# Second attention of a two-layer cross-attention kernel: score pieces, the maximum's transposition, the turned output and the projection placed elsewhere, and low parts of the probabilities moved from VectorE to GpSimd

## The chip, the core and the metric

The kernel runs on one core of one Trainium2 chip. The metric is the device time of one execution in microseconds. The engines are named as in the profile: PE (TensorE), DVE (VectorE), ACT (ScalarE), POOL (GpSimd), SP (the queue that issues the transfers). Each engine works through its own instructions in order; between engines only semaphores (`wait_ge`, `then_inc`) hold anything back.

## The reference, cut to what matters

Two layers are computed. The first has self-attention, cross-attention with 16 heads of 8, and a feed-forward part; nothing of it is changed. The second is one more cross-attention, over the same context, and it is the part that the change touches:

```
h = layernorm(x)                          # x: 16 batches x 56 queries x 128
Q = (h @ Wq).reshape(B, NQ, 16, 64)
K = (context @ Wk).reshape(B, NC, 16, 64) # context: 16 batches x 1500 keys x 96
V = (context @ Wv).reshape(B, NC, 16, 64)
attn = softmax(einsum('bihd,bjhd->bhij', Q, K)) * 64 ** -0.5
vals = einsum('bhij,bjhd->bihd', attn, V).reshape(B, NQ, 1024)
out = x + vals @ Wo + bo
```

## The kernel before

The second attention runs batch by batch, 16 batches. The 16 heads' queries (56 each) make 896 columns, 7 tiles of 128; the keys are 12 chunks of 125, two chunks to a group `g`, six groups and a seventh round for what is left. Wq and Wk are folded together beforehand, and Wv and Wo too, so that the context's 96 columns stand for keys and values both. `over_pairs` runs the batches in pairs, `par` 0 and 1 (a loop on the chip from the third batch to the fourteenth, the rest written out).

For batch `b`, PE does these things in a group `g`:

- **Scores** of two chunks, `score(i, par, u)`, four of them (L1319, L1320, 448 columns each), into four banks of PSUM, and then `score_rests` (L1328), which adds the last rows and subtracts the maximum. `score` u waits until ACT has read what lay in its bank (`n_exp`), four scores earlier.
- ACT takes the exponential from PSUM (L1423) into `P1`, four chunks deep.
- The **low part** of a chunk's probabilities, `Pl`, is `P1` minus its upper 16 bits. Before, POOL makes it (L1300) for all chunks but 3, 7 and 11, which are DVE's (L1521). Either reads two tensors that lie in SBUF.
- **Values** of the two chunks of the group before, `values` (L1346 to L1348, 21 products per chunk), which wait for the low part (`n_low_p`, `n_low_d`).
- Beside it, **pieces** for the next batch: its scores are computed once roughly (L1033, 21 pieces of 128 x 500), only for their maxima, which DVE reduces (L1042). Two PSUM banks alternate, so a piece waits until the piece two before it is reduced (`n_red`). Row `g` of the table `PLACES` says where pieces stand in group `g`: after the first, second and third score, after the rests, and after each chunk's values.

At a batch's end (g = 6) DVE makes the next batch's maximum (`negate_maximum`, L1487 to L1495: a reduction and four tiny instructions on 128 x 7, all in SBUF, one after the other), PE transposes it (`turn_maximum`, L1373), then does the values of chunks 10 and 11; DVE lays the maximum into the next batch's queries (L1501), which that batch's fourth score waits for.

The finished batch's output is divided by its sums by DVE (`finish_batch`, L1453 and L1457, at the start of the next batch), turned by PE (`turn_output`, L1357, two parts), kept by ACT (L1440) and DVE (L1466), and, once for two batches (`par` 0), projected by PE (`project`, L1365, 48 products) and finished by DVE (`finish_tile`, L1471 and L1475). POOL also makes the low part of the next batch's context once per batch (`cNl`, L1304), after chunk 3's place.

Of the kernel before, what the change touches and what calls it, by code (L numbers as in the profile page):

```python
# [37 lines left out]
SK, DC = 1500, 96  # L38
# [74 lines left out]
def program(nc, table, x, ctx_768, w_qkv, b_qkv, w_so, b_so, w_q, b_q, w_k, b_k, w_v, b_v, w_co, b_co,  # L113
            w1, b1, w2, b2, w3, b3, ln_g, ln_b, Wq, Wk, Wv, Wo, bo, gamma, beta, out):
    with ExitStack() as ctx:
# [1119 lines left out]
        mn1 = sb_in(late, "mn1", [128, MR])  # L1235
# [6 lines left out]
        PLACES = [(0, 0, 0, 0, 0, 0), (0, 0, 0, 0, 0, 1), (1, 1, 1, 1, 1, 1), (1, 0, 1, 1, 1, 1), (1, 0, 1, 1, 1, 1), (1, 1, 1, 1, 0, 0), (0,) * 6]  # L1242
# [3 lines left out]
        n_mready, n_mturned, n_mlaid = (sem(n) for n in ("n_mready", "n_mturned", "n_mlaid"))  # L1246
# [4 lines left out]
        low_on_dve = [c % 4 == 3 for c in range(NC)]  # L1251
# [13 lines left out]
        with nc.Block() as block:  # L1265
# [42 lines left out]
            def _(pe):  # L1308
# [23 lines left out]
                def values(i, par, c, tiles):  # L1332
                    n = i * 2 + par
                    if tiles[0] == 0:
                        if low_on_dve[c]:
                            pe.wait_ge(n_low_d, n * DV + sum(low_on_dve[:c + 1]))
                        else:
                            pe.wait_ge(n_low_p, n * (NC - DV) + c + 1 - sum(low_on_dve[:c + 1]))
                        if c == 0:
                            pe.wait_ge(n_cnl, n + 1)  # L1340
                            wait_for(pe, n_on, n)
# [10 lines left out]
                def turn_output(n, k):  # L1352


                    pe.wait_ge(n_on, n + 1)
                    for t in range(4 * k, min(4 * k + 4, QT)):
                        mm = pe.transpose(PS[0:DC, W1[k], (t % 4) * 128:(t % 4 + 1) * 128], On[:, t, :], ident)  # L1357
                    mm.then_inc(n_oturned, 1)
# [10 lines left out]
                def turn_maximum(i, par):  # L1369
                    n = i * 2 + par + 1  # L1370
                    pe.wait_ge(n_mready, n + 1)
                    for first in (32, 96):
                        mm = pe.matmul(PS[first:first + MR, W1[0], 0:128], mn1[:], ident, start=True, stop=True)  # L1373
                    mm.then_inc(n_mturned, 1)

                def body(i, par):
# [10 lines left out]
                    for g in range(NG + 1):  # L1387
                        if has_1 and g == NG:
                            turn_maximum(i, par)
                        if has_b and g < NG:  # L1390
                            for j in range(2 * GC):
                                score(i, par, 2 * GC * g + j)
                                if has_old and g == 1 and j < 2:
                                    turn_output(b - 1, j)
                                if j < 3:
                                    pieces(g, j)
                            score_rests(par, g)
                        pieces(g, 3)
                        for j in range(GC):
                            if has_b and g > 0:  # L1400
                                values(i, par, GC * (g - 1) + j, tuple(range(QT)))
                            pieces(g, 4 + j)
                        if has_b and has_old and par == 0 and g == 1:
                            project(i - 1)
# [42 lines left out]
            def _(dve):  # L1447
                def finish_batch(n):
# [5 lines left out]
                    dve.wait_ge(n_r, n * 2 + 2)  # L1454
                    wait_for(dve, n_oturned, n * 2)
                    for k in range(2):
                        m = nc.vector.scalar_tensor_tensor(out=On[:, 4 * k:4 * k + 4 - k, :], in0=o[k][:, :, 0:DC], scalar=SCALE1,  # L1457
                                                           in1=spread(r7[:, 4 * k:4 * k + 4 - k], 2, DC), op0=ALU.mult, op1=ALU.mult)
                    m.then_inc(n_on, 1)
# [17 lines left out]
                def body(i, par):  # L1477
# [6 lines left out]
                    def negate_maximum():  # L1484
# [9 lines left out]
                        nc.vector.tensor_scalar(mn1[:, 0:QT], mh1[:], -1.0, None, ALU.mult)  # L1494
                        nc.vector.tensor_tensor(mn1[:, QT:], mh1[:], mt1[:], ALU.subtract).then_inc(n_mready, 1)  # L1495
# [10 lines left out]
                    for g in range(NG + 1):  # L1506
# [4 lines left out]
                        if has_b and has_old and par == 0 and g == 2:  # L1511
                            finish_tile(i - 1)
# [4 lines left out]
                        if has_b and g >= 2 and g % 2 == 0:  # L1517
# [38 lines left out]
```

## Time and profile before

| | us |
|---|---|
| median of 3 runs | 1120.08 (1120.08 to 1121.38) |
| the profiled execution | 1121.01, of it the span of the profile 1119.1 |
| feed-forward part and preparation | 480 to 583 |
| second attention, batches | 583 to 1107 |
| its last output and projection | 1107 to 1119 |
| mean granted clock of PE over the span | 0.969 of full speed |

Every start time is counted in microseconds from the start of the span. A matmul's duration in the trace is that of one passing through the array, and successive ones overlap: for a stream of them the distance of two starts is what one costs. Idle time that the trace gives before a matmul is counted from the end of the one before, so start-to-start it is some 0.2 us more. A row with "x4" merges four instructions in a row on that engine.

### The profile page before, as it was taken

To read this page: it belongs to the slowest core of one execution; us is meant where nothing else is said; L and a number is where in the kernel's file an instruction comes from. 1 tells how busy PE (TensorE), PEld (TensorE's weight loads), DVE (VectorE), ACT (ScalarE), POOL (GpSimd) and SP (SyncE) were. 2 spreads that over 40 slices of the span, in tenths; PEclk is the share of its full clock that TensorE was granted. 3 is DMA by queue.
4 is the path that set the end of the run, shared out by engine and by line. 5 is a ranking of instruction groups with operands and counts; after the bars stand their busy time and mean duration, and the time that the engine had idled before them with its cause. 6 is when DMAs were issued, how large, how long until landed. Compare 5 with 4: busy or idle time off the path is not lost. (4 is left out here: it accounts for less than half of the span.)

```text
span 1119.1 us, 31806 instructions
## 1 busy us (share of the span) xinstructions
PE 1016.2 (91%) x12092; PEld 704.7 (63%) x12092; DVE 752.5 (67%) x1409; ACT 543.3 (49%) x1139; POOL 402.6 (36%) x290
## 2 busy tenths in 40 slices
PE   5977899999999999889678999999999999999997
PEld 2652577777677776646326676766766666676666
DVE  4646778887888788221786667677676767766662
ACT  2533577677776776631443434333443442444442
POOL 4821121112111123020115545445555544655543
PEclk9988899999999999989799999999999999999998
DMA  3501444444344533020023122222022222112200
GB/s 111 136 1 63 141 140 132 130 150 138 123 130 146 145 107 90 19 80 1 0 76 93 45 77 75 54 75 71 27 72 74 59 68 75 48 48 73 57 2 4
DMA packets 54605, 88.31 MB, mean 79 GB/s; under 512 B 10850, under 2 KB 39348, under 8 KB 54548
## 3 DMA queue, kind: packets, MB, share of 16 engines
q1 hardware_dynamic: 54548, 87.52, 26.6%
q8 instruction: 40, 0.66, 0.3%
q14 instruction: 17, 0.14, 0.0%
HBM read 57.27 MB, written 21.96 MB: 71 GB/s over the span
## 5 line engine op out<-in xcount | busy, mean ns | idle before, releaser
L1423 ACT ACTIVATE P<-PS 125x448 f32<-125x448 f32 x384 | 177.8, 550 | 309.2 <-PE PS L1328 309.2
L1300 POOL TENSOR_TENSOR Pl<-P 125x896 f16<-125x896 f32 x144 | 240.7, 1686 | 239.9 <-ACT P L1423 239.5
L1042 DVE TENSOR_REDUCE m<-PS 128x1 f32<-128x500 f32 x336 | 216.1, 675 | 92.7 <-PE PS L1033 91.0
L922 DVE TENSOR_REDUCE m_part<-PS 128x1 f32<-128x500 f32 x336 | 210.5, 672 | 55.2 <-PE PS L824 53.7
L900 ACT ACTIVATE Pb<-PS 125x448 f32<-125x448 f32 x384 | 186.1, 549 | 19.8 <-PE PS L799 18.8
L1346 PE MATMUL PS<-cNh,P 125*128 125x97 f16 x1344 | 186.3, 208 | 1.1 <-POOL Pl L1300 1.1
L1348 PE MATMUL PS<-cNh,Pl 125*128 125x97 f16 x1344 | 185.7, 207 | 0.0
L1347 PE MATMUL PS<-cNl,P 125*128 125x96 f16 x1344 | 185.5, 206 | 0.0
L1319 PE MATMUL PS<-qA,kA 128*125 128x448 f16 x384 | 136.7, 356 | 8.5 <-ACT P L1423 8.2
L1347 PEld LDWEIGHTS PS<-cNl,P 125*128 125x128 bf16 x1344 | 132.0, 98 | 11.5
L1346 PEld LDWEIGHTS PS<-cNh,P 125*128 125x128 bf16 x1344 | 131.5, 98 | 11.3 <-issue 9.5
L775 POOL TENSOR_TENSOR Qst<-Qspace,tab 96x224 f16<-96x224 f32 (+1 forms) x64 | 33.7, 556 | 290.7 <-DVE Qst L962 281.6
L824 PE MATMUL PS<-KH,Qmx 128*128 128x500 f16 x336 | 129.8, 388 | 8.7 <-DVE m_part L922 4.2
L1033 PE MATMUL PS<-kA,qA 96*128 96x500 f16 x336 | 126.9, 378 | 9.3 <-DVE m L1042 7.8
L1320 PE MATMUL PS<-qB,kB 128*125 128x448 f16 x384 | 134.9, 351 | 0.0
L1348 PEld LDWEIGHTS PS<-cNh,Pl 125*128 125x128 f16 x1344 | 131.4, 98 | 0.0
L799 PE MATMUL PS<-Qst,Kst 110*125 110x224 f16 x768 | 110.9, 263 | 4.9 <-DMA Kst<-k_halves 2.1
L799 PEld LDWEIGHTS PS<-Qst,Kst 110*125 110x125 f16 x768 | 87.8, 137 | 30.4 <-ACT Pb L900 7.7
L810 PE MATMUL PS<-Pb,Vst 125*32 125x112 f32 x3072 | 93.3, 262 | 0.0
L810 PEld LDWEIGHTS PS<-Pb,Vst 125*32 125x32 f32 x3072 | 70.4, 109 | 19.6 <-issue 15.4
L1319 PEld LDWEIGHTS PS<-qA,kA 128*125 128x125 f16 x384 | 52.2, 136 | 30.1 <-ACT P L1423 15.4
L1521 DVE TENSOR_TENSOR Pl<-P 125x896 f16<-125x896 f32 x48 | 61.2, 1276 | 14.0 <-ACT P L1423 14.0
(170 smaller groups left out, 1522.7 us busy)
## 6 DMA issues: line engine op xcount, KB each, us to landing
Kst<-k_halves SPq DMA_DIRECT2D x144, 125.0 KB, 2.8
k_halves<-KH SPq DMA_DIRECT2D x16, 750.0 KB, 3.3
cx<-in_ctx SPq DMA_DIRECT2D x16, 562.5 KB
d_cx<-in_ctx SPq DMA_DIRECT2D x16, 562.5 KB
kB<-c_halves SPq DMA_DIRECT2D x32, 187.5 KB, 3.3
c_halves<-cHi SPq DMA_DIRECT2D x16, 281.2 KB, 2.7
c_halves<-cLo SPq DMA_DIRECT2D x16, 281.2 KB, 3.0
kA<-c_halves SPq DMA_DIRECT2D x16, 281.2 KB, 3.2
```

Source lines behind the costliest of these rows:

```text
L799: mm = pe.matmul(PS[0:KC, u % 3, (g % 2) * 224:(g % 2 + 1) * 224], Kst[:, par, g, c * KC:(c + 1) * KC], Qst[:, par, g, :], start=True, sto ...
L810: mm = pe.matmul(PS[32 * (p % 4):32 * (p % 4) + 32, OB, (p // 4) * TP:(p // 4 + 1) * TP], Vst[:, par, c, p, :], Pb[:, c % NPB, p * TP:(p + ...
L900: nc.scalar.activation(Pb[:, c % NPB, half * HALF:(half + 1) * HALF], PS[0:KC, u % 3, 0:HALF], ACT.Exp, scale=SCALE0).then_inc(exp_done, 1)
L922: nc.vector.tensor_reduce(m_part[:, t, part:part + 1], PS[:, 6 + k % 2, 0:SP], AX.X, ALU.max).then_inc(s_reduced, 1)
L1042: nc.vector.tensor_reduce(m21[:, t, part:part + 1], PS[:, banks[k % 2], 0:SP], AX.X, ALU.max).then_inc(n_red, 1)
L1300: nc.gpsimd.tensor_tensor(Pl[:, c % NP], P1[:, c % NP], high, ALU.subtract).then_inc(n_low_p, 1)
L1319: pe.matmul(o, kA[:, par, at], qA[:, par, cols], start=True, stop=False)
L1320: pe.matmul(o, kB[:, par, at], qB[:, par, cols], start=False, stop=True)
L1346: pe.matmul(o, high, cNh[:, par, c, :], start=(c == 0 and t % 4 == 0), stop=False, skip_group_check=True)
L1347: pe.matmul(o[:, 0:DC], high, cNl[:, par, c, :], start=False, stop=False, skip_group_check=True)
L1348: mm = pe.matmul(o, Pl[:, c % NP, cols], cNh[:, par, c, :], start=False, stop=(c == NC - 1), skip_group_check=True)
L1423: nc.scalar.activation(P1[:, c % NP, half * HALF:(half + 1) * HALF], PS[0:KC, u % 4, 0:HALF], ACT.Exp).then_inc(n_exp, 1)
```

## The change

Seven things are changed, all in the second attention:

1. DVE keeps only chunk 3's low part; those of chunks 7 and 11 are POOL's.
2. `PLACES` for groups 2 and 3 are exchanged: group 2 has five pieces and group 3 six.
3. `turn_maximum` is one product with 128 rows of output in place of two with 14 each; `mn1` is therefore 128 x 2 x 64, cleared once, and the last two tiny instructions of `negate_maximum` write 128 x 2 x 7.
4. `turn_output` stands between group 0's rests and group 1's first score, both parts together, in place of within group 1's scores.
5. `finish_batch` signals each half of the output for itself, and `turn_output` waits for its own half.
6. `project` stands after the values of chunk 0, in place of after chunk 1's and the first piece.
7. `finish_tile` stands in group 1 ahead of the first piece's reduction, in place of in group 2.

```diff
-        mn1 = sb_in(late, "mn1", [128, MR])
+        mn1 = sb_in(late, "mn1", [128, 2, 64])
-        PLACES = [(0, 0, 0, 0, 0, 0), (0, 0, 0, 0, 0, 1), (1, 1, 1, 1, 1, 1), (1, 0, 1, 1, 1, 1), (1, 0, 1, 1, 1, 1), (1, 1, 1, 1, 0, 0), (0,) * 6]
+        PLACES = [(0, 0, 0, 0, 0, 0), (0, 0, 0, 0, 0, 1), (1, 0, 1, 1, 1, 1), (1, 1, 1, 1, 1, 1), (1, 0, 1, 1, 1, 1), (1, 1, 1, 1, 0, 0), (0,) * 6]
-        low_on_dve = [c % 4 == 3 for c in range(NC)]
+        low_on_dve = [c == 3 for c in range(NC)]
...
                 def turn_output(n, k):
-                    pe.wait_ge(n_on, n + 1)
+                    pe.wait_ge(n_on, n * 2 + k + 1)
...
                     pe.wait_ge(n_mready, n + 1)
-                    for first in (32, 96):
-                        mm = pe.matmul(PS[first:first + MR, W1[0], 0:128], mn1[:], ident, start=True, stop=True)
-                    mm.then_inc(n_mturned, 1)
+                    pe.matmul(PS[:, W1[0], 0:128], mn1[:].rearrange("p a c -> p (a c)"), ident, start=True, stop=True).then_inc(n_mturned, 1)
...
                                 score(i, par, 2 * GC * g + j)
-                                if has_old and g == 1 and j < 2:
-                                    turn_output(b - 1, j)
                                 if j < 3:
                                     pieces(g, j)
                             score_rests(par, g)
+                        if has_b and has_old and g == 0:
+                            turn_output(b - 1, 0)
+                            turn_output(b - 1, 1)
                         pieces(g, 3)
                         for j in range(GC):
                             if has_b and g > 0:
                                 values(i, par, GC * (g - 1) + j, tuple(range(QT)))
+                            if has_b and has_old and par == 0 and g == 1 and j == 0:
+                                project(i - 1)
                             pieces(g, 4 + j)
-                        if has_b and has_old and par == 0 and g == 1:
-                            project(i - 1)
...
-                    dve.wait_ge(n_r, n * 2 + 2)
                     wait_for(dve, n_oturned, n * 2)
                     for k in range(2):
-                        m = nc.vector.scalar_tensor_tensor(...)
-                    m.then_inc(n_on, 1)
+                        dve.wait_ge(n_r, n * 2 + k + 1)
+                        nc.vector.scalar_tensor_tensor(...).then_inc(n_on, 1)
...
-                        nc.vector.tensor_scalar(mn1[:, 0:QT], mh1[:], -1.0, None, ALU.mult)
-                        nc.vector.tensor_tensor(mn1[:, QT:], mh1[:], mt1[:], ALU.subtract).then_inc(n_mready, 1)
+                        nc.vector.tensor_scalar(mn1[:, :, 32:32 + QT], spread(mh1[:], 1, 2), -1.0, None, ALU.mult)
+                        nc.vector.tensor_tensor(mn1[:, :, 32 + QT:32 + MR], spread(mh1[:], 1, 2), spread(mt1[:], 1, 2), ALU.subtract).then_inc(n_mready, 1)
...
-                        if has_b and has_old and par == 0 and g == 2:
+                        if has_b and has_old and par == 0 and g == 1:
                             finish_tile(i - 1)
...
-                        if has_b and g >= 2 and g % 2 == 0:
+                        if has_b and g == 2:
```

At a batch's end, inside the loop, DVE's instructions stood like this before (`m` are the piece maxima, `mt`, `mh`, `mn` the steps of the maximum, `Pl` the low part of chunk 11, `qC` the next batch's queries):

```order
L1042 TENSOR_REDUCE m<-PS 128x1
L1487 TENSOR_REDUCE mt<-m 128x7
L1489 TENSOR_SCALAR mt<-mt 128x7
L1491 CAST mh<-mt 128x7
L1494 TENSOR_SCALAR mn<-mh 128x7
L1495 TENSOR_TENSOR mn<-mh,mt 128x7
L1521 TENSOR_TENSOR Pl<-P 125x896
L1501 TENSOR_TENSOR qC<-PS,tab 14x512 x2
```

and now like this:

```order
L1042 TENSOR_REDUCE m<-PS 128x1
L1488 TENSOR_REDUCE mt<-m 128x7
L1490 TENSOR_SCALAR mt<-mt 128x7
L1492 CAST mh<-mt 128x7
L1495 TENSOR_SCALAR mn<-mh 128x2x7
L1496 TENSOR_TENSOR mn<-mh,mt 128x2x7
L1502 TENSOR_TENSOR qC<-PS,tab 14x512 x2
```

The low part of chunk 11 has left DVE, where it stood behind the maximum's four tiny instructions. On POOL the second attention's first two batches read so (`Pl` the low parts, `cNl` that of the context; the sign says which kernel):

```order
 L1300 TENSOR_TENSOR Pl<-P 125x896 x3
 L1304 TENSOR_TENSOR cNl<-d_cx,cNh 125x1152
-L1300 TENSOR_TENSOR Pl<-P 125x896 x9
+L1300 TENSOR_TENSOR Pl<-P 125x896 x11
 L1304 TENSOR_TENSOR cNl<-d_cx,cNh 125x1152
-L1300 TENSOR_TENSOR Pl<-P 125x896 x6
+L1300 TENSOR_TENSOR Pl<-P 125x896 x8
```

The run behind each `cNl` is longer by two, the low parts of chunks 7 and 11, and chunk 11's now stands directly behind chunk 10's. On PE the start of a batch in the loop, from group 0's rests on, stood so before (`On` is the divided output, turned):

```order
L1328 MATMUL PS<-qC,kC 125x448 x4
L84 REGISTER_ALU
L1319 MATMUL PS<-qA,kA 125x448
L1320 MATMUL PS<-qB,kB 125x448
L1357 MATMUL PS<-tab,On 96x128 x4
L84 REGISTER_ALU
L1319 MATMUL PS<-qA,kA 125x448
L1320 MATMUL PS<-qB,kB 125x448
L1357 MATMUL PS<-tab,On 96x128 x3
```

and now:

```order
L1328 MATMUL PS<-qC,kC 125x448 x4
L1355 ISA
L1357 MATMUL PS<-tab,On 96x128 x4
L1355 REGISTER_ALU
L1357 MATMUL PS<-tab,On 96x128 x3
L84 REGISTER_ALU
L1319 MATMUL PS<-qA,kA 125x448
L1320 MATMUL PS<-qB,kB 125x448
```

The seven transpositions now stand ahead of group 1's first score.

## Rows read from the trace of the kernel before

**Rows 1.** Windows: PE, PEld, DVE, ACT, POOL busy us (x instructions), PEclk, DMA share, GB/s.
```profile
583.00:1107.00 524.00, 492.17 (x6004) 351.39 (x6004) 350.51 (x605) 210.75 (x461) 277.47 (x160) 1.00 0.21 60
```

**Rows 2.** Waits of PE, all of the span: us in total, times, longest.
```profile
PE PS L1373 <- DVE mn L1495: 18.5, 16, 2.5
...
PE PS L1319 <- ACT P L1423: 8.2, 16, 0.5
PE PS L1033 <- DVE m L1042: 7.8, 21, 0.7
```

**Rows 3.** Timeline of DVE at one batch's end (start, us, engine, line, instruction).
```profile
744.95 1.42 DVE L1489 TENSOR_SCALAR mt<-mt 128x7 f32<-128x7 f32 x1
746.40 0.17 DVE L1491 CAST mh<-mt 128x7 f16<-128x7 f32 x1
...
746.69 0.16 DVE L1495 TENSOR_TENSOR mn<-mh,mt 128x7 f32<-128x7 f16 x1
```

**Rows 4.** Timeline of POOL, then of ACT, at that end and the next start.
```profile
744.66 1.68 POOL L1300 TENSOR_TENSOR Pl<-P 125x896 f16<-125x896 f32 x1 [1.93 <-ACT P L1423]
752.28 3.32 POOL L1300 TENSOR_TENSOR Pl<-P 125x896 f16<-125x896 f32 x2 [5.94 <-ACT P L1423]
...
743.61 1.85 ACT L1423 ACTIVATE P<-PS 125x448 f32<-125x448 f32 x4 [3.40 <-PE PS L1328]
```

**Rows 5.** Timeline of PE, same stretch.
```profile
746.90 0.40 PE L1373 MATMUL PS<-tab,mn 128*14 128x128 f32 x4 [1.09 <-DVE mn L1495]
747.24 0.22 PE L1346 MATMUL PS<-cNh,P 125*128 125x97 f16 x1
...
751.82 0.40 PE L1319 MATMUL PS<-qA,kA 128*125 128x448 f16 x1 [0.54 <-ACT P L1423]
...
752.25 0.60 PE L1357 MATMUL PS<-tab,On 128*96 128x128 f32 x4
...
755.68 0.21 PE L1346 MATMUL PS<-cNh,P 125*128 125x97 f16 x1
```

**Rows 6.** Lines L1489 and L1521: duration ns min/median/max, first and last start.
```profile
L1489 DVE TENSOR_SCALAR mt<-mt x16: 171/1415/1417, 582.4 to 1076.7; 128x7 f32<-128x7 f32 x16
L1521 DVE TENSOR_TENSOR Pl<-P x48: 1079/1082/2107, 595.2 to 1104.1; 125x896 f16<-125x896 f32 x48
```

**Rows 7.** Timeline of DVE, POOL and PE in that next batch, group 2.
```profile
758.87 2.10 DVE L1521 TENSOR_TENSOR Pl<-P 125x896 f16<-125x896 f32 x1
...
757.73 2.30 POOL L1304 TENSOR_TENSOR cNl<-d_cx,cNh 125x1152 f16<-125x1152 f32 x1 [0.23 <-ACT cNh L1427]
...
761.62 0.39 PE L1033 MATMUL PS<-kA,qA 96*128 96x500 f16 x1 [0.68 <-DVE m L1042]
```

**Rows 8.** Timeline of POOL and DVE at 18 us, and line L358.
```profile
18.30 3.57 POOL L358 TENSOR_TENSOR Kbd<-SKT,tab 128x896 f32<-128x896 f32 x2 [9.27 <-DVE SKT L430]
...
18.66 1.67 DVE L434 SCALAR_TENSOR_TENSOR wkv<-wkv 97x256 f16<-97x256 f32 x1
...
L358 POOL TENSOR_TENSOR Kbd<-SKT,tab x16: 1689/1692/1866, 18.3 to 58.1; 128x896 f32<-128x896 f32 x16
```

**Rows 9.** Timeline in a batch with a projection: PE, then DVE.
```profile
725.53 0.35 PE L1320 MATMUL PS<-qB,kB 128*125 128x448 f16 x1
725.88 0.39 PE L1033 MATMUL PS<-kA,qA 96*128 96x500 f16 x1
...
726.07 0.29 DVE L1475 TENSOR_TENSOR Z<-Y,X 112x128 f32<-112x128 f32 x1 [0.24 <-DVE Y L1471]
```

**Rows 10.** Timeline of DVE behind the last batch.
```profile
1107.36 0.92 DVE L1457 SCALAR_TENSOR_TENSOR On<-PS,r 128x384 f32<-128x384 f32 x2
```

**Rows 11.** Windows around long gaps of PE, columns as in rows 1.
```profile
560.00:583.00 23.00, 17.50 (x48) 5.23 (x46) 21.73 (x41) 8.24 (x15) 0.00 (x0) 1.00 0.18 49
...
95.00:112.00 17.00, 10.90 (x28) 2.71 (x27) 14.32 (x23) 4.05 (x5) 3.75 (x5) 0.77 0.30 106
...
1107.00:1119.00 12.00, 6.35 (x56) 5.89 (x55) 3.04 (x10) 1.08 (x4) 0.00 (x0) 0.67 0.03 7
```

More of the change, by code:

```diff
@@ L1245, in program @@
         n_cn, n_cnl = sem("n_cn"), sem("n_cnl")
-        n_mready, n_mturned, n_mlaid = (sem(n) for n in ("n_mready", "n_mturned", "n_mlaid"))
+        n_mzero, n_mready, n_mturned, n_mlaid = (sem(n) for n in ("n_mzero", "n_mready", "n_mturned", "n_mlaid"))
         n_exp, n_low_d, n_low_p, n_pv = (sem(n) for n in ("n_exp", "n_low_d", "n_low_p", "n_pv"))
@@ L1340, in values @@
                             pe.wait_ge(n_cnl, n + 1)
-                            wait_for(pe, n_on, n)
+                            wait_for(pe, n_on, n * 2)
                     for t in tiles:
@@ L1447, in _ @@
             def _(dve):
+                nc.vector.memset(mn1[:], 0.0).then_inc(n_mzero, 1)
+                dve.wait_ge(n_mzero, 1)
                 def finish_batch(n):
@@ L1453, in finish_batch @@
                         nc.vector.reciprocal(r7[:, 4 * k:4 * k + 4 - k].unsqueeze(2), o[k][:, :, DC:DC + 1]).then_inc(n_r, 1)
-                    dve.wait_ge(n_r, n * 2 + 2)
                     wait_for(dve, n_oturned, n * 2)
                     for k in range(2):
-                        m = nc.vector.scalar_tensor_tensor(out=On[:, 4 * k:4 * k + 4 - k, :], in0=o[k][:, :, 0:DC], scalar=SCALE1,
-                                                           in1=spread(r7[:, 4 * k:4 * k + 4 - k], 2, DC), op0=ALU.mult, op1=ALU.mult)
-                    m.then_inc(n_on, 1)
+                        dve.wait_ge(n_r, n * 2 + k + 1)
+                        nc.vector.scalar_tensor_tensor(out=On[:, 4 * k:4 * k + 4 - k, :], in0=o[k][:, :, 0:DC], scalar=SCALE1,
+                                                       in1=spread(r7[:, 4 * k:4 * k + 4 - k], 2, DC), op0=ALU.mult, op1=ALU.mult).then_inc(n_on, 1)
                 def split_old(i, par, k):
```

## The prediction

> **What bounds the kernel now.** I read the windows first, then PE's waits, then the timeline of one batch's end and the next one's start. Through the 524 us of the second attention PE is busy 492 us, at the full granted clock (1.00), while DVE has 351 and POOL 277 [rows 1]. So PE's stream bounds the stretch, and the time changes where PE stands still, or where its stream gets shorter. The list of its waits names three places that the change touches [rows 2]: the maximum's transposition (16 times, 18.5 us), the first score of group 1 behind ACT's exponential (16 times, 8.2 us), and a piece behind DVE's reduction (21 times, 7.8 us). Everything is at one of these.
>
> Why does the first one exist? At a batch's end DVE subtracts a constant from 128 x 7 numbers (L1489). That took 1.42 us, from 744.95 to 746.37 [rows 3], but 171 ns the first time, at 582.4, when POOL did nothing; the median of its 16 is 1415 ns [rows 6]. POOL's low part of chunk 10 ran from 744.66 to 746.34 [rows 4]: DVE's tiny instruction ended 0.03 us after POOL's. The 1.42 us are not work, they are a wait for POOL. The reader is to see the same at two other places. DVE's low part of chunk 3 takes 1082 ns as a rule and 2107 at most [rows 6]; the one at 758.87 took 2.10, and POOL's `cNl` beside it ran until 760.03 [rows 7]. And at 18.66 a DVE instruction with two inputs in SBUF took 1.67 us: it ended at 20.33, soon after the first of two POOL instructions in a row (18.30, 3.57 us both) must have ended, and before the second did [rows 8]. One of POOL's L358 took 1866 ns against a median of 1692 [rows 8]: DVE, having waited, was let in between, and POOL's second was held up a little.
>
> **The change part by part.** All against the profiled execution, 1121.01 us (span 1119.1), which is 0.93 over the median 1120.08.
>
> *Chunk 11's low part to POOL.* Its input is there early: ACT ends all four exponentials at 743.61 + 1.85 = 745.46 [rows 4]. So POOL starts it as soon as chunk 10's ends, 746.34, and two in a row take 3.32 us [rows 4]; this one ends at about 744.66 + 3.32 = 747.98, say 748.02 with L1489 let in between. Before, POOL was idle from 746.34 until 752.28 [rows 4], and in that idle time DVE did the cast and the two instructions that write `mn` (746.40 to 746.85), and PE its transposition at 746.90 [rows 3, 5]. Now these meet a busy POOL. L1489 gets in at 746.37 as before; the cast comes 0.03 us later [rows 3], POOL has started again, and the cast ends at 748.02 + 0.03 = 748.05. From its end to the end of L1495 is 746.85 - 746.57 = 0.28 us [rows 3], so `mn` is ready at 748.33 and PE starts at 748.38 instead of 746.90: **+1.48 us a batch**. Bounds: no row shows that cast beside POOL. If it and the scalar instruction slip through, the last one, L1496, still has two SBUF inputs as L1521 has, whose wait is shown [rows 6, 7]; it would end at about 748.05 in place of 746.85: +1.2. If L1489 is not let in between but has to wait for both, the chain starts at 748.02 and needs 746.85 - 746.37 = 0.48: +1.65. If nothing waits, 0 (a rival below). I take 1.48, because the cast is nearest to L1489: one input, both sides in SBUF, seven elements. PE has nothing ahead of this wait to do: chunk 10's and 11's values and the whole next batch stand behind it on PE, and ACT's exponentials behind those. DVE's laying of the maximum and its low part no longer stand between, but the fourth score that waits for them is more than 2 us behind, so their leaving DVE gives nothing. The same goes for chunk 7's low part: PE does not wait in groups 4 and 5, before or after.
>
> [...]
>
> *One transposition for two.* From the first product's start to chunk 10's first value is 747.24 - 746.90 = 0.34 us for four passes [rows 5]; with two passes some 0.11 less, and loading 128 columns instead of 14 takes back a little: **-0.10 us a batch** (0 to -0.12).
>
> So a batch's end costs +1.38, fifteen times (the transposition ahead of the first batch meets an idle POOL, 171 ns): **+20.7 us**, between 15 x 1.08 = 16.2 and 15 x 1.55 = 23.3. In the last batch there is no maximum, but chunk 11's low part, 1.66 us behind chunk 10's, is later than chunk 10's values (21 products, 0.91 us) need it: **+0.7**.
>
> *The turned output before group 1.* PE waited 0.54 us ahead of group 1's first score and then spent 7 x 0.11 = 0.77 us on transpositions between scores [rows 5]; with restart costs the gap was 0.65. Now the transpositions lie in it: chunk 11's values end at 747.24 + 1.82 = 749.06 [rows 5], DVE's divisions (0.92 us [rows 10], 0.5 behind that) are done by 750.5, and PE comes at 751.82 - 0.6 = 751.2. PE is 0.65 us early at the end of group 1's scores. What is late next is POOL: the low parts of chunks 0 and 1 ran 752.28 to 755.60 [rows 4] and start with ACT's exponential, which didn't move. In a batch without a projection chunk 1's values began at 755.68 [rows 5], 0.08 after that; they can begin at 755.65 now. So there the gain is **0.03**. In a batch with a projection its 2.7 us now stand between chunk 0's values and chunk 1's and cover that wait; the gain of 0.65 stays.
>
> *finish_tile in group 1.* After the projection a piece came 0.35 us after the score ahead of it in place of 0.19 [rows 9]: 0.17 us of waiting for Y. Now Y is made beside chunk 1's values. But Z reads two SBUF tensors [rows 9], and beside POOL's `cNl` it can wait a microsecond; the reductions behind it are late then, and piece 2 by some 0.1. Together a batch with a projection gains 0.65 + 0.17 - 0.1 = **0.7, seven times: -4.9 us** (bounds 0.4 and 0.82).
>
> *Five pieces in group 2.* In batches without a projection PE waited 0.84 us start to start (0.68 idle) at 761.62, since L1521 had stood waiting for `cNl` [rows 7], and 0.05 at an earlier piece. ACT's copy for `cNl` now starts 0.6 us earlier, and `cNl` goes behind three low parts in a row (755.60 + 1.68 = 757.28) until about 759.5; L1521 comes at 759.2, waits 0.3 and ends at 760.5, and chunk 3's values want it at 760.7. With five pieces instead of six the last one, at 761.6, needs a reduction that ends at 761.1. Group 3's sixth piece finds DVE caught up. So the wait goes: **-0.89, with the 0.03 -0.92, seven times (the last batch has no pieces): -6.4 us** (bounds 0.3 and 0.95).
>
> *The tail.* The first half of the last output is signalled 0.4 us earlier of its 0.92 [rows 10]: **-0.4**. The clearing of `mn1` is hidden: it is 128 elements during the first batch's preparations.
>
> Sum: 20.7 + 0.7 - 4.9 - 6.4 - 0.4 = **+9.7**. From 1121.01 that is 1130.7; against the median, **1129.8 us**.
>
> **The rivals.**
> - *The tiny instructions slip past POOL*, because DVE is served at each handover or these sizes don't contend. For it: L1489 did get in behind a POOL instruction. Against: it got in only where POOL ended, and L1521 with two inputs never ran beside POOL's work. Then the end of a batch gives -0.10 x 15 = -1.5, and the sum is -1.5 + 0.7 - 4.9 - 6.4 - 0.4 = -12.5: 1107.6. It decides from the point where the added wait is below 0.76 us a batch. Chance 0.10.
> - *The gains are eaten as well*: low parts come later still for group 2 (POOL has 11 of them and `cNl` now, three in a row at the start), so L1521 waits behind `cNl` as before and nothing is won in batches without a projection, half in the others: 20.7 + 0.7 - 2.5 - 0.4 = +18.5, 1138.6. Chance 0.07.
> - *The clock falls.* PE's idle time per batch's end grows from 1.09 [rows 5] to some 2.5 us. For it: in 95 to 112 us, with PE busy 10.90 of 17, the mean granted clock was 0.77, and behind the last batch 0.67 [rows 11]. Against: in 560 to 583, with PE busy 17.50 of 23, it was 1.00 [rows 11], and a batch here would be busy nine tenths. If it fell for some 3.4 us each time, half of that is lost: 15 x 1.7 = +25, 1155. Chance 0.03.
> - *It nets to nothing*: only L1496 waits, and the earlier parts give their upper bounds: 16.2 + 0.7 - 5.7 - 6.7 - 0.6 = +3.9, 1124. Chance 0.08, a third of it within no change.
>
> **How the numbers follow.** The forecast has 0.72. Its own range is 1125.5 to 1133; the tail's projection runs at a clock that is partly halved (0.67), which may shift by a microsecond or two either way. The range reaches down to the case of a part wait and up towards eaten gains: 1123 to 1138. A measurement of this kernel can tell 0.2% (2.2 us) from no change. Faster is 0.12, no change 0.04, slower 0.84.
>
> **What would show it.** Right: after, L1492 (the cast) or what is behind it takes 1.4 to 1.7 us and ends with POOL's second low part; PE's wait ahead of L1372 sums to about 18.5 + 15 x 1.48 = 40 us; the wait at group 1's first score is gone in all batches but the first; in batches without a projection a new wait of 0.6 us for POOL stands at chunk 1's values, and the piece at 761.62 no longer waits. Wrong: the cast and L1496 stay at 0.17 us beside a busy POOL (then 1107), or PEclk below 1.00 between 583 and 1107 (then over 1140), or L1522 in group 2 still at 2.1 us in batches without a projection.

## The result: slower by 2.5 %, and the profile after

| | before | after |
|---|---|---|
| median us | 1120.08 (1118.76 to 1121.38, 4 runs) | 1148.06 (1147.05 to 1149.92, 4 runs) |
| ratio | 1 | 1.0252 [1.0233, 1.027] |
| profiled execution, its span | 1121.01, 1119.1 | 1147.42, 1145.5 |
| mean granted clock of PE | 0.969 | 0.957 |

The forecast was 1129.8 with a range to 1138, so the sign is right and the size is not: +28.0 us in place of +9.7. The views of after, in the order in which I read them. First PE's waits, which answer to [rows 2]:

```profile
PE PS L1372 <- DVE mn L1496: 40.4, 16, 2.7
...
PE PS L1346 <- POOL Pl L1300: 4.7, 11, 0.7
...
PE PS L1033 <- DVE m L1042: 3.1, 14, 0.7
```

The wait ahead of the transposition has gone from 18.5 to 40.4 us, where 40 was forecast. At group 1's first score a single wait of 0.5 us for ACT is left (16 waits, 8.2 before), and the pieces wait less (3.1 against 7.8). The timelines of one batch's end, DVE, POOL and PE, answer to [rows 3 to 5]:

```profile
751.43 0.17 DVE L1488 TENSOR_REDUCE mt<-m 128x7 f32<-128x21 f32 x1
751.64 1.42 DVE L1490 TENSOR_SCALAR mt<-mt 128x7 f32<-128x7 f32 x1
753.09 1.60 DVE L1492 CAST mh<-mt 128x7 f16<-128x7 f32 x1
754.73 0.17 DVE L1495 TENSOR_SCALAR mn<-mh 128x14 f32<-128x14 f16 x1
754.81 0.17 DVE L1496 TENSOR_TENSOR mn<-mh,mt 128x14 f32<-128x14 f16 x1
```
```profile
751.35 3.32 POOL L1300 TENSOR_TENSOR Pl<-P 125x896 f16<-125x896 f32 x2 [1.93 <-ACT P L1422]
```
```profile
755.04 0.49 PE L1372 MATMUL PS<-tab,mn 128*128 128x128 f32 x2 [2.53 <-DVE mn L1496]
755.36 0.21 PE L1346 MATMUL PS<-cNh,P 125*128 125x97 f16 x1
```

POOL's two low parts run from 751.35 to 754.67. L1490 ends at 753.06, about where the first must have ended (751.35 + 1.68 = 753.03); the cast, which took 0.17 us before, takes 1.60 and ends at 754.69, 0.02 after POOL's second. PE stands idle for 2.53 us in place of 1.09. L1490 and the cast wait for semaphores of DVE's own steps alone, and for none of POOL's, so "only semaphores hold anything back" does not hold for these two engines here: L1490 took 1.42 us and the cast 1.60, where each took 0.17 with no POOL instruction beside it (L1490 in e6, the cast in before). So far this is the mechanism of the prediction. The windows show what it left out; they answer to [rows 1]:

```profile
583.00:1133.00 550.00, 506.46 (x5943) 367.30 (x5943) 337.95 (x571) 207.89 (x459) 325.60 (x192) 0.96 0.20 57
719.50:722.90 3.40, 3.40 (x35) 3.00 (x33) 1.80 (x6) 0.00 (x0) 0.00 (x0) 0.50 0.43 120
722.90:753.00 30.10, 29.61 (x356) 21.13 (x354) 18.86 (x31) 13.11 (x29) 18.81 (x12) 1.00 0.11 34
```

The mean granted clock of the second attention is 0.96, not 1.00. The second row is 3.4 us right behind a batch's end: PE busy throughout, granted clock 0.50; the third, the rest of that batch, is at 1.00. Such a stretch of 3.4 us goes with 12 of the 15 transpositions at a batch's end in the profiled execution: it begins between the transposition's start and 1.2 us behind it. (One more begins behind the last batch, where before had one too.) By estimate, with half of each 3.4 us lost at 0.50, that is 12 x 1.7 = 20.4 us. At three ends with the same standstill, at 755.04, 894.99 and 1034.92, the clock did not fall; they lie four batches apart.

### The profile page after: what moved, and what is told of

It reads as the page before. It is cut to its first block and busy times, and to the rows that moved or that the text cites. A ratio compares the mean times of both kernels' runs of the same rounds, so it can differ in the third digit from the quotient of the medians.

```text
span 1145.5 us, 31762 instructions
## 1 busy us (share of the span) xinstructions
PE 1029.2 (90%) x12060; PEld 719.2 (63%) x12060; DVE 741.2 (65%) x1378; ACT 542.0 (47%) x1139; POOL 452.8 (40%) x322
## 5 line engine op out<-in xcount | busy, mean ns | idle before, releaser
L1300 POOL TENSOR_TENSOR Pl<-P 125x896 f16<-125x896 f32 x176 | 291.6, 1679 | 224.1 <-ACT P L1422 224.1
L1346 PE MATMUL PS<-cNh,P 125*128 125x97 f16 x1344 | 200.5, 215 | 4.7 <-POOL Pl L1300 4.7
L1348 PE MATMUL PS<-cNh,Pl 125*128 125x97 f16 x1344 | 200.1, 214 | 0.0
L1347 PE MATMUL PS<-cNl,P 125*128 125x96 f16 x1344 | 199.7, 213 | 0.0
L900 ACT ACTIVATE Pb<-PS 125x448 f32<-125x448 f32 x384 | 185.9, 547 | 19.5 <-PE PS L799 18.5
L1347 PEld LDWEIGHTS PS<-cNl,P 125*128 125x128 bf16 x1344 | 137.6, 102 | 12.3
L1346 PEld LDWEIGHTS PS<-cNh,P 125*128 125x128 bf16 x1344 | 136.9, 102 | 13.0 <-POOL Pl L1300 11.7
L1319 PE MATMUL PS<-qA,kA 128*125 128x448 f16 x384 | 139.3, 363 | 0.8 <-ACT P L1422 0.5
L1320 PE MATMUL PS<-qB,kB 128*125 128x448 f16 x384 | 137.2, 357 | 0.0
L1348 PEld LDWEIGHTS PS<-cNh,Pl 125*128 125x128 f16 x1344 | 136.8, 102 | 0.0
L1320 PEld LDWEIGHTS PS<-qB,kB 128*125 128x125 f16 x384 | 53.8, 140 | 20.3
```

The source lines that it names most:

```text
L900: nc.scalar.activation(Pb[:, c % NPB, half * HALF:(half + 1) * HALF], PS[0:KC, u % 3, 0:HALF], ACT.Exp, scale=SCALE0).then_inc(exp_done, 1)
L1300: nc.gpsimd.tensor_tensor(Pl[:, c % NP], P1[:, c % NP], high, ALU.subtract).then_inc(n_low_p, 1)
L1319: pe.matmul(o, kA[:, par, at], qA[:, par, cols], start=True, stop=False)
L1320: pe.matmul(o, kB[:, par, at], qB[:, par, cols], start=False, stop=True)
L1346: pe.matmul(o, high, cNh[:, par, c, :], start=(c == 0 and t % 4 == 0), stop=False, skip_group_check=True)
L1347: pe.matmul(o[:, 0:DC], high, cNl[:, par, c, :], start=False, stop=False, skip_group_check=True)
```

## The experiments

The distance from one maximum's transposition to the next gives the length of a batch, in us, for batches with a projection (`par` 0) and without. It is the finest measure here, since the runs of one kernel differ by up to 8 us (e1: 1103.42 to 1111.71) while these lengths repeat within 0.03 us in the loop as long as the clock doesn't fall:

| kernel | with | without | median us | ratio to before |
|---|---|---|---|---|
| before | 34.16 | 32.21 | 1120.08 | 1 |
| after | 36.45 | 34.33 (32.71 without a fall) | 1148.06 | 1.0252 |
| e1 chunk 11 back to DVE | 33.43 | 31.28 | 1108.65 | 0.9908 [0.9891, 0.9925] |
| e2 before, chunk 11 to POOL | 35.6 to 37.1 | 35.25 | 1161.88 | 1.0372 [1.0355, 1.0389] |
| e4 transposition later | 33.96 | 31.81 | 1116.84 | 0.9971 [0.9961, 0.9982] |
| e10 one product in the gap | 34.86 | 32.71 | 1128.69 | 1.0074 [1.0051, 1.0097] |
| e7 e1, output's places of before | 34.16 | 31.62 | 1115.59 | 0.9959 [0.9947, 0.9972] |
| e8 e1, pieces' places of before | 33.81 | 31.67 | 1114.00 | 0.9949 [0.9936, 0.9962] |
| e6 e1, chunk 10 on DVE too | 32.97 | 30.82 | 1100.52 | 0.9814 [0.9797, 0.9831] |
| e11 e6, some of chunk 1 too | 32.97 | 30.59 | 1098.07 | 0.9806 [0.9786, 0.9827] |

The theory: chunk 11's low part on POOL makes DVE's cast wait (+1.48 a batch), and PE's longer standstill makes the clock fall. The rivals: the fall has another source, or the gains of the other edits are missing.

**e1 and e2, the one move undone, and the one move alone.** Of after, then of before:

```diff
-        low_on_dve = [c == 3 for c in range(NC)]
+        low_on_dve = [c in (3, 11) for c in range(NC)]
...
-                        if has_b and g == 2:
+                        if has_b and g in (2, 6):
```


> The changed kernel with chunk 11's low part given back to DVE, behind the maximum's tiny instructions; all other edits stay. Theory A (GpSimd's low part of chunk 11, right behind chunk 10's, holds up the maximum's cast by 1.43 us, and the longer standstill of TensorE lets the granted clock fall): the cast is back at 0.17 us, TensorE's wait ahead of the maximum's transposition is back from 40.4 to 18.5 us in total, the granted clock is 1.00 from 583 us on, and the time is about 1109 us (1120 less the 11 us that the other edits were worked out to give). Theory B (the clock falls because of another of the edits, such as the 128-row transposition or the pieces' places): the wait is back, but the clock stays at 0.96 there and the time is about 1131 us. Theory C (GpSimd is overloaded with eleven low parts): chunk 7's alone keeps half of the loss, about 1130 us.


```diff
-        low_on_dve = [c % 4 == 3 for c in range(NC)]
+        low_on_dve = [c in (3, 7) for c in range(NC)]
...
-                        if has_b and g >= 2 and g % 2 == 0:
+                        if has_b and g in (2, 4):
```


> The kernel before with one thing changed: chunk 11's low part goes to GpSimd, chunks 3 and 7 stay on VectorE. Theory A: the cast takes 1.6 us in 15 batches, TensorE's wait ahead of the transposition goes from 18.5 to about 40 us, which gives 1120 + 22 + 0.7 = 1143 us, and the clock falls at nearly every batch's end too, another 20 us or so: about 1163 us. Theory B: the wait grows but the clock stays at 1.00, because other edits let it fall: 1143 us. Theory C: nearly nothing, 1120 to 1125 us.

Measured 1108.65 and 1161.88. The cast's line, PE's waits and the windows of e1:

```profile
L1492 DVE CAST mh<-mt x16: 172/173/174, 580.0 to 1063.1; 128x7 f16<-128x7 f32 x16
...
PE PS L1372 <- DVE mn L1496: 18.9, 16, 2.7
...
583.00:1090.00 507.00, 485.74 (x5922) 349.32 (x5922) 332.08 (x586) 207.74 (x459) 299.19 (x175) 1.00 0.21 61
```

and of e2:

```profile
L1491 DVE CAST mh<-mt x16: 174/1606/1607, 584.0 to 1116.6; 128x7 f16<-128x7 f32 x16
...
PE PS L1373 <- DVE mn L1495: 40.0, 16, 2.5
...
583.00:1150.00 567.00, 511.01 (x6004) 368.00 (x6004) 356.93 (x597) 211.64 (x461) 303.82 (x176) 0.96 0.19 56
```

The move alone gives the before kernel the long cast, the 40 us of waiting and the clock of 0.96; without it none of the three is there, and the other six edits, with chunk 7's low part still on POOL, gain 0.9 %. The whole loss comes with chunk 11's move.

**e3, e5, e9: fill the gap, keep the cast late.** Products whose results nobody reads (e3's are added to 97 columns beside the accumulators, in their bank, which hold no result) stand ahead of the transposition's wait: 54 of 97 columns, 12 of 448 columns, or three float32 ones of 448 columns.

```diff
+                    if inside(i, par, 0):
+                        pe.wait_ge(n_exp, (i * 2 + par) * 2 * NC + 2 * NC - 3)
+                        for _ in range(3):
+                            pe.matmul(PS[0:KC, 0, 0:HALF], ident[0:KC, 0:KC], P1[:, 9 % NP, 0:HALF], start=True, stop=True)
                     pe.wait_ge(n_mready, n + 1)
```


> The changed kernel with 54 more products (128 x 97, into columns of a PSUM bank that nobody reads) on TensorE ahead of the wait for the maximum, 54 x 0.043 = 2.3 us a batch, so that TensorE works through most of the 2.7 us in which it stood still. Nothing else moves. Theory A: the added work costs nothing, the cast still takes 1.6 us, the granted clock is 1.00 from 583 us on, and the time is 1148 less 13 falls of 3.4 us at half speed (1.7 us each) = about 1126 us, within 1124 to 1130. Theory B (the clock falls for another reason): the clock stays at 0.96 and the time at 1148 us or above.

> The changed kernel with 12 long extra products (96 x 448, into a score bank that is free then, result unread) ahead of TensorE's wait for the maximum: 12 x 0.19 = 2.3 us a batch, in 12 instructions in place of the 54 of the run before. With 54, the falls of the clock at the batches' ends were gone, but TensorE stood still 3.3 to 3.6 us for nothing the profile names at the loop's first score, five times, and the clock fell there. Theory A (the standstill makes the clock fall; the new one came from the longer program in the loop): no such standstill with 12, the clock 1.00 from 583 us on, the wait for the maximum below 0.5 us each, and 1148 - 22 = about 1126 us (1124 to 1130). Theory B (the clock falls for another reason): 1148 us.

> The changed kernel with three extra float32 products (125 x 448, 0.76 us each by the float32 products of the feed-forward part, result unread) ahead of TensorE's wait for the maximum: 2.3 us a batch in three instructions. The loop's program on TensorE then has 883 instructions in place of 875; with 901 and 983 it was loaded anew in each pass and TensorE stood still for about 4 us. Theory A (the standstill lets the clock fall; the loop's size is what cost the other two runs their gain): no loading in the loop, the clock 1.00 from 583 us on, 1148 - 22 = about 1126 us. Rival (883 is already too long): loading and 5 standstills of 4 us again, about 1150 us. Theory B (the clock falls for another reason): 1148 us with the clock at 0.96.

Measured 1154.51, 1159.56 and 1159.48: all slower than after. The first two are a plain miss; e9 went the way of its rival (a loop that is too long, about 1150), and beyond it. The falls at the batches' ends were gone, but something new had come. PE's waits, a row of PE's timeline, and the page's instruction queue of e9:

```profile
PE PS L1319 <- issue: 20.6, 5, 4.5
...
792.83 0.63 PE L1319 MATMUL PS<-qA,kA 128*125 128x448 f16 x1 [4.43 <-issue]
...
q8 instruction: 85, 1.39, 0.6%
```

At the loop's first score PE stands still five times, named only "issue": 3.6 to 4.5 us in e9, up to 4.0 in e5 and up to 3.6 in e3. The clock falls at each: over the 12 us behind the standstill its mean is 0.75 to 0.88. The queue that carries instructions has 85 packets (87 in e3) where before and after have 40. The times of these three therefore say nothing of the gap. The lengths of their other batches do: 34.86 and 32.71, with PE idle for at most 0.26 us ahead of the transposition and no fall (clock 1.00). Why the five standstills are there became a question of its own (below).

**e10, the gap filled with one instruction.** As e9, with one product (0.76 us):

```diff
-                        for _ in range(3):
+                        for _ in range(1):
```


> As the run with three float32 products, but one: TensorE's standstill ahead of the maximum is cut from 2.5 to about 1.75 us. If its length is what counts and 1.75 is too short for a fall, about 1126 us and the clock at 1.00; if it still falls as often, 1148 us; anything between says that part of the batches' ends fall. The version with the values first had two gaps, together nearly as long, and no fall before the last batch.

Measured 1128.69. The windows and PE's timeline of e10:

```profile
583.00:1117.00 534.00, 500.07 (x5960) 354.50 (x5960) 340.67 (x580) 210.34 (x462) 326.05 (x192) 1.00 0.20 59
...
753.00 0.49 PE L1376 MATMUL PS<-tab,mn 128*128 128x128 f32 x2 [1.71 <-DVE mn L1500]
```

The cast still waits and PE's useful work stands as long as in after (a batch without a fall is 32.71 us in both), but the idle stretch is cut to 1.71 us, and the clock stays at 1.00. So the falls cost 1148.06 - 1128.69 = 19.4 us (12 of 1.6), and the rest of the loss, +0.74 % or 8.6 us, is what was forecast (+9.7).

**e4, the transposition behind chunk 10's values,** where the standstill is cut in two:

```diff
-                        if has_1 and g == NG:
+                        if has_1 and g == NG and not has_b:
                             turn_maximum(i, par)
...
                                 values(i, par, GC * (g - 1) + j, tuple(range(QT)))
+                            if has_1 and has_b and g == NG and j == 0:
+                                turn_maximum(i, par)
```


> The changed kernel with the values of chunk 10 put ahead of the maximum's transposition on TensorE; they wait only for chunk 10's low part. The cast still waits for GpSimd (1.6 us). Theory A: 0.91 us of work a batch moves into the standstill (15 x 0.91 = 13.6 us) and cuts it into two waits of 0.7 and 1.1 us, so the clock does not fall: 1148 - 22 - 13.6 = about 1112 us. If the clock falls all the same, because the standstill is as a whole still 1.8 us: about 1134 us. Theory B: 1134 us.

Measured 1116.84 (8 runs). PE's timeline at a batch's end, its waits and the windows of e4:

```profile
741.47 0.22 PE L1346 MATMUL PS<-cNh,P 125*128 125x97 f16 x1 [0.59 <-POOL Pl L1300]
743.41 0.49 PE L1372 MATMUL PS<-tab,mn 128*128 128x128 f32 x2 [0.87 <-DVE mn L1498]
...
PE PS L1372 <- DVE mn L1498: 15.8, 16, 2.7
...
PE PS L1346 <- POOL Pl L1300: 13.3, 26, 0.7
...
583.00:1100.00 517.00, 489.74 (x5959) 351.23 (x5956) 337.69 (x570) 207.77 (x459) 325.59 (x191) 1.00 0.20 60
```

The cast is as late as in after, but PE's idle gap of 2.53 us has become two of 0.59 and 0.87, with a chunk's values between them; the clock is at 1.00. This says the same as e10 by another edit. The late cast is then half hidden, and the change beats before by 0.3 %.

**e6 and e11: keep POOL away from the maximum.** e6 is e1 with chunk 10's low part on DVE too; in e11 chunk 1's as well, in batches without a projection, ahead of the turned output's low parts (the lines that count the low parts for the waits are left out):

```diff
...
-                        if has_b and g in (2, 6):
-                            c = GC * g - 1
+                        for c in {2: (3,), 6: (10, 11)}.get(g, ()) if has_b else ():
```


> As the run with chunk 11's low part on DVE (1108.65 us), and chunk 10's on DVE too, both behind the maximum's tiny instructions. Theory A: no GpSimd work is left beside the tiny instructions, so the constant's subtraction takes 0.17 us in place of 1.42, the maximum is ready before chunk 9's values end and TensorE's wait for it (1.26 us a batch start to start) goes; in its place chunk 10's values wait some 0.6 us for DVE. A batch's end gets 0.48 us shorter, 15 times, the last batch 0.6: 1108.65 - 7.8 = about 1101 us. Rival: DVE, with 1.08 us more per batch, is now late for the laying of the maximum, and the next batch's fourth score waits: 1106 to 1112 us.


```diff
...
+                        if has_b and par == 1 and g == 1:
+                            dve.wait_ge(n_exp, (b * NC + 1 + 1) * 2)
+                            nc.vector.tensor_tensor(Pl[:, 1], P1[:, 1], P1[:, 1].bitcast(BF16)[:, 1::2], ALU.subtract).then_inc(n_low_d, 1)
```


> As the run with the low parts of chunks 10 and 11 on DVE (1100.5 us), and chunk 1's on DVE too in batches without a projection, ahead of the turned output's low parts. DVE waits until GpSimd's chunk 0 ends and is done 0.94 us later, 0.65 us before GpSimd would be with chunk 1. TensorE's wait of 0.56 us ahead of chunk 1's values (start to start) goes in eight batches: 1100.5 - 4.5 = about 1096 us. Rival: the turned output's low parts come 1.3 us later, and the first piece behind them waits as long as was won: 1100.5 us or a little more.

Measured 1100.52 and 1098.07. A batch's end in e6, DVE and PE:

```profile
740.26 0.17 DVE L1490 TENSOR_SCALAR mt<-mt 128x7 f32<-128x7 f32 x1
...
740.84 2.09 DVE L1521 TENSOR_TENSOR Pl<-P 125x896 f16<-125x896 f32 x2
```
```profile
740.98 0.49 PE L1372 MATMUL PS<-tab,mn 128*128 128x128 f32 x2
741.98 0.22 PE L1346 MATMUL PS<-cNh,P 125*128 125x97 f16 x1 [0.51 <-DVE Pl L1521]
```

With POOL silent, L1490 takes its own 0.17 us and the transposition doesn't wait at all. What is late next is chunk 10's low part, 0.51 us. That gains 0.46 us a batch over e1. In e11 the wait at chunk 1's values is gone, but the first piece then comes 0.34 us late (0.17 idle), which is a part of what the rival said: batches without a projection gain 0.23, and by their ratios the two kernels can't be told apart. Both beat before (-1.9 %) and after.

**e7 and e8: the places, one half back at a time,** both from e1. e7 puts the turned output, the projection and `finish_tile` where they stood before; e8 the old `PLACES`.

```diff
                                 score(i, par, 2 * GC * g + j)
+                                if has_old and g == 1 and j < 2:
+                                    turn_output(b - 1, j)
...
-                        if has_b and has_old and g == 0:
-                            turn_output(b - 1, 0)
-                            turn_output(b - 1, 1)
...
-                        if has_b and has_old and par == 0 and g == 1:
+                        if has_b and has_old and par == 0 and g == 2:
                             finish_tile(i - 1)
```


> As the run with chunk 11's low part on DVE (1108.65 us), but the turned output, the projection and the finished tile stand where they stood before the change. Theory A as worked out in the prediction: batches with a projection lose 0.7 us each, seven times, those without next to nothing (chunk 1's values wait for GpSimd either way): 1108.65 + 5 = about 1113.5 us. Rival (the early turned output gains in every batch): + 0.65 x 15 + 1.2 = 1119 us.


```diff
-(1, 0, 1, 1, 1, 1), (1, 1, 1, 1, 1, 1), (1, 0, 1, 1, 1, 1)
+(1, 1, 1, 1, 1, 1), (1, 0, 1, 1, 1, 1), (1, 0, 1, 1, 1, 1)
```


> As the run with chunk 11's low part on DVE (1108.65 us), but with six pieces in group 2 and five in group 3 as before the change. Theory A: chunk 3's low part still waits for the context's low part on GpSimd, but 0.3 us in place of 1.0, as that starts earlier; a piece then waits about 0.45 us in batches without a projection: 1108.65 + 3 = about 1111.7 us. Rival (the earlier start alone cured the wait, the places do nothing): 1108.7 us. Rival (the places alone cured it): + 0.84 x 7 = 1114.5 us.

Measured 1115.59 and 1114.00, each some 2 us over what was expected. By batch lengths the output's places are worth 0.73 us with a projection and 0.34 without one, the pieces' places 0.38 and 0.39, for seven pairs some 7.5 and 5.4 us where 5 and 3 were expected. In e7, without a projection, chunk 3's low part waits for a later `cNl` (it takes 1.80 us, where 1.08 is the median) and its values come 0.31 late for it; in e8, with one, a piece comes 0.40 us late behind Z, which takes 1.13 (0.29 in before).

**e12, e13, e14: how long may the loop be?** e1 with 5 or 12 of e3's products a batch, and e10 with two float32 products:

```diff
-                        for _ in range(54):
+                        for _ in range(5):
```
```diff
-                        for _ in range(5):
+                        for _ in range(12):
```
```diff
-                        for _ in range(1):
+                        for _ in range(2):
```


> The kernel with chunk 11's low part on DVE (1108.65 us) and five short extra products (128 x 97, 0.2 us together, result unread) per batch ahead of TensorE's wait of 1.26 us for the maximum, which they hide in. The loop's program on TensorE gets ten instructions longer, and nothing else changes. If the length of the loop's program is what brought the standstill of 4 us at its start (all three versions with 883 or more instructions in it had it, none with 879 or fewer): five such standstills, the clock falls behind each, about 85 instruction packets in place of 40, and 1108.65 + 5 x (4 + 1.7 to 3) = about 1138 us. Rival (that standstill came from TensorE reaching the loop's end without having waited): no standstill, 40 packets, 1108.7 us.

> As the run with five short extra products a batch (1107.96 us, nothing loaded anew), but twelve: 0.5 us a batch, which still hides in the wait of 1.26 us. By the traces the loop's program on TensorE then has some 906 instructions (892 with five; 896, 908 and 990 in the three runs with the standstill at its start). If the loop's length decides, with its limit between 892 and 896: standstills of 4 us at the loop's start, 85 instruction packets, about 1108 + 5 x (4 + 1.7 to 3) = 1135 us. Rival (it comes when TensorE reaches the loop's end without having waited there; here it still waits 0.7 us): 40 packets and 1108 us.

> The changed kernel with two extra float32 products a batch: 892 instructions in the loop by the trace's count, and TensorE's standstill ahead of the maximum down to about 1 us. If the loop's length decides: nothing loaded anew, the clock at 1.00 from 583 us on, and the same 1128.7 us as with one product, since both hide in the standstill. Rival (TensorE has to wait a good while near the loop's end): somewhere between 1129 and 1159 us.

Measured 1107.96 (six runs, five of 1105.72 to 1113.79 and one of 1129.43), 1141.67 and 1164.80. PE's waits of e13, then of e14, and e14's instruction queue:

```profile
PE PS L1319 <- issue: 21.8, 5, 4.6
```
```profile
PE PS L1319 <- issue: 21.6, 5, 4.6
...
q8 instruction: 85, 1.39, 0.5%
```

I counted PE's instructions, without its weight loads, in one pass of the loop in the trace. Kernels with 882 (after, e1), 884 (before), 888 (e10) and 892 (e12) run with 40 packets; those with 896 (e9), 906 (e13), 908 (e5) and 990 (e3) with 85 to 87 and five standstills. e14 misses: it has 892 as e12 has, and has the standstills. Its other batches are 34.86 and 32.71, as e10's, with no fall at their ends. So the kernels with the standstills take 31 to 36 us more here (e9 and e14 against e10, e13 against e1).

The records of the instruction queue show what goes with them. Between 711 and 1071 us, where the loop's last five passes run, it brings nothing in after. In e9 it brings nine packets in each of the five passes (the 45 that e9 has more), and one of them starts 0.2 to 0.3 us into each of the five standstills. I read this as a longer loop that is loaded anew in each pass while PE stands at the pass's start; the traces show the packets and the standstills together, but name no releaser ("issue"). The rival, that it comes when PE reaches the loop's end without having waited enough, fails: PE is idle for 0.96 us ahead of the transposition in e14, which has the standstills, and for 0.88 in e12, which has none. What exactly decides it, and in what unit, was not shown: e12 and e14 both have 892.

## Why the prediction was right and wrong

- **The batch's end, +1.48 us: right.** The distance from L1490's end to the transposition grew by 1.45 us, since the cast took 1.60 us; the last two instructions took 0.17 each and didn't wait. The distance of batch lengths between e10 and e1 is 1.43, in both kinds. The bound of +1.2, for a cast that slips through, did not come: the cast, with one input, waited, and ended 0.02 us behind POOL's second low part.
- **One transposition for two, -0.10: mis-sized.** From its start to chunk 10's first value it is 755.36 - 755.04 = 0.32 us against 0.34: -0.02, a miss of some 1.2 us in all. The 0.11 us less for two passes was the author's estimate, and no run parts it from what the 128 columns take back.
- **Batches with a projection -0.7, without -0.92: right in the sum.** e1 against before is -0.73 and -0.93, of which the transposition has 0.02. The split among edits was not quite right: e7 shows 0.34 us, not 0.03, from the output's places in batches without a projection, since with an earlier `cNl` chunk 3's low part took 1.28 us in place of 1.80; and e8 shows 0.38 from the pieces in batches with one, where no wait of that kind was foreseen. Each of two edits can take the same wait away, and the gain shows in whichever is undone.
- **The last batch and the tail, +0.7 - 0.4 = +0.3.** From the last transposition to the end it is 40.55 us in before and 40.80 in e10, both with some 8 us at a granted clock of 0.50 behind the last batch: +0.25. The two terms by themselves were not measured.
- **The new waits.** Chunk 1's values do wait for POOL (0.56 us start to start, forecast 0.6), L1522 takes 1.28 us in group 2 (forecast 1.3), Z 1.12 beside POOL (forecast about one more).
- **The failed step: the clock's fall, put at nothing in the sum and at 0.03 among the rivals.** Its price was close (1.7 us a fall; a batch with a fall is 36.45 - 34.86 = 1.59 longer), but it was ruled out by the row 560 to 583 at full clock [rows 11]. In place of no fall the clock fell at 12 of 15 ends, 19.4 us, and its sign of being wrong came true (PEclk below 1.00 before 1107, over 1140). The row was weak evidence twice over. It has one standstill of 2.5 us in a setting of its own, and no row of before showed a dense stream with a gap as long as the 2.5 us that the prediction had itself worked out. The 3.4 us of a fall stood in none of its rows either; they are the author's assumption there, and the runs showed them only later (in after 0.50 from 719.50 to 722.90). And the row is one outcome of two. The same standstill ahead of the first batch's transposition, 2.7 us in after and in the thirteen experiments made from it, went with a fall in the profiled executions of six of these 14 kernels (e5, e6, e7, e8, e12, e13), though what runs up to there is all but the same. e6 has it so:

```profile
582.94 0.49 PE L1372 MATMUL PS<-tab,mn 128*128 128x128 f32 x2 [2.73 <-DVE mn L1496]
...
583.92:590.75 6.83, 6.56 (x22) 2.81 (x20) 0.93 (x2) 2.11 (x5) 4.50 (x3) 0.50 0.88 226
```

That an unknown of this size had no place in the range is the error: sum +9.7, falls +19.4, together +29 against +28 measured. One small slip beside it: the first rival turns the sign below an added wait of 11.0 / 15 + 0.10 = 0.83 us a batch, not 0.76.

Shown: that the moved low part makes the cast late and brings the falls with it (e1, e2), and that a shorter gap at the same late cast does away with them (e10, e4). Not shown: why three ends kept their clock (in e2 it was three as well, but other ones), and why the standstill at 583 us is followed by a fall in some executions only.

## What to carry to other kernels

A wait that grew cost more than its length here, where PE then stood still in one piece (1.43 us of wait brought 1.6 us more at 12 of 15 ends): before moving work that lengthens a standstill of a dense stream, price the clock's fall as well, and if the wait can't be avoided, put a piece of PE's own work into its middle, as e4 does (gaps of 0.59 and 0.87 us, clock 1.00). One stretch at full clock behind a like gap is no proof that the clock holds: behind 2.7 us at the first batch it held in eight of 14 kernels and fell in six. The chain of tiny dependent VectorE instructions on SBUF lost to GpSimd once for each GpSimd instruction beside it (twice in after, 1.42 and 1.60 us; once in before and e1, 1.42; not at all in e6, where each took 0.17), so keep GpSimd silent over such a chain, not only less busy. And compare the length of a loop's program before reading an experiment that adds instructions to it (here 896 and more, and once 892, went with five standstills of up to 4.6 us, 882 to 892 otherwise with none).

## What the runs showed of the hardware that I had not expected

- In after a gap of 2.45 to 2.53 us, once in some 35 us of otherwise busy PE, went with 3.4 us at a granted clock of 0.50 at 12 of 15 ends; gaps of 1.71 us (e10), 1.09 us (before), or 0.59 and 0.87 us with 0.9 us of work between them (e4), went with none in the batches.
- A gap of 2.7 us behind the sparser work ahead of 583 us (PE busy 17.13 of 23 us in after) went with 6.8 to 10.2 us at 0.50 in the profiled executions of six of 14 kernels that have the same instructions there.
- In the kernels whose loop on PE had grown from 882 instructions to 896 or more (in e14, though not in e12, to 892) the instruction queue's packets went from 40 to 85 or 87, in e9 by nine in each of five passes, and PE stood still for up to 4.6 us at the start of these passes. The profile calls it only "issue"; the packet count is what told the kernels apart.
- Beside two GpSimd instructions back to back (751.35 to 754.67 in after) L1490 took 1.42 us and ended at 753.06, about the first's end; the cast, next in its chain and started 0.03 us later, took 1.60 us and ended at 754.69, 0.02 behind the second's.
